# Feed-forward: the convolution's right tap as a diagonal float32 matmul at the head of TensorE's step, and VectorE scaling one chunk ahead instead of two

## What is computed

```python
def bit_linear(x, w):                 # act_quant: 8 bits by row; weight_quant: -1, 0, 1
    xq = act_quant(x)
    wq = weight_quant(w)
    return jnp.einsum('bsd,hd->bsh', xq, wq)

h = bit_linear(layernorm(x), w1)      # 512 -> 2048
h = depthwise_conv1d(h.transpose(0, 2, 1), conv_w, conv_b)   # 3 taps along the sequence, padding 1
h = silu(h.transpose(0, 2, 1))
x = x + bit_linear(h, w2)             # 2048 -> 512
```

## Time and profile before

| | |
|---|---|
| median of 3 runs | 3316.15 us (3313.43 to 3318.39) |
| the profiled execution: time / span | 3314.49 us / 3312.7 us |
| granted TensorE clock, mean over the span | 0.893 |
| busy in the span: TensorE / VectorE / ScalarE / GpSimd | 2574.8 / 1853.1 / 1203.9 / 910.4 us |
| rounds 0 to 8 of this feed-forward | about 649 to 1160 us of the span |

### The profile page before, as it was taken

One profiled execution on the slowest core, in us unless ns is written; L12 is line 12 of the kernel. 1 busy time (PEld: TensorE's weight loads), 2 busy tenths in 40 slices (PEclk: granted clock), 3 DMA queues, 4 the chain that ended last, 5 costly groups with the idle time before them and its releaser, 6 DMA issues. The chain is left out here.

```text
span 3312.7 us, 44462 instructions
## 1 busy us (share of the span) xinstructions
PE 2574.8 (78%) x14146; PEld 1327.2 (40%) x14147; DVE 1853.1 (56%) x2672; ACT 1203.9 (36%) x1807; POOL 910.4 (27%) x741
## 2 busy tenths in 40 slices
PE   8377777356666658888887509999999999999970
PEld 4244444122232234444444204444444444444430
DVE  4477776789889676676664642223233333332225
ACT  2233333287887655555554421111111111111110
POOL 0010100066776711111111170005055311350017
PEclk9788888678888879999998859999999999999995
DMA  9560000100000020000000361003033211220018
GB/s 217 119 238 8 7 8 5 51 0 1 1 0 0 0 63 9 9 8 8 11 8 14 117 225 42 32 32 108 32 108 103 76 62 50 89 95 32 32 52 274
DMA packets 118043, 194.11 MB, mean 59 GB/s; under 512 B 55264, under 2 KB 55264, under 8 KB 117456
## 3 DMA queue, kind: packets, MB, share of 16 engines
q1 hardware_dynamic: 92607, 102.96, 11.4%
q0 software_dynamic: 25360, 90.21, 8.0%
HBM read 122.65 MB, written 70.48 MB: 58 GB/s over the span
## 5 line engine op out<-in xcount | busy, mean ns | idle before, releaser
L1806 PE MATMUL e_gate_up<-weights,e_x_t 128*128 x3456 | 772.2, 380 | 1.4 <-ACT e_x_t L1860 1.4
L1806 PEld LDWEIGHTS e_gate_up<-weights,e_x_t 128*128 128x128 bf16 x3456 | 332.8, 98 | 377.4 <-issue 5.1
L1893 DVE TENSOR_TENSOR e_mid<-e_gate,e_gate_up 128x512 f32<-128x512 f32 x144 | 98.9, 687 | 645.8 <-ACT e_gate L1866 645.8
L1826 PE MATMUL e_out<-weights,e_mid_t 128*128 x1728 | 384.7, 379 | 1.1 <-DVE e_mid_t L1906 1.1
L1866 ACT ACTIVATE e_gate<-e_gate_up 128x512 f32<-128x512 f32 x144 | 86.0, 597 | 684.6 <-PE e_gate_up L1806 684.6
L559 PE MATMUL a_turn<-a_wo,a_mixed_t 128*128 128x512 bf16 (+1 forms) x1024 | 284.9, 435 | 2.4 <-DVE a_mixed_t L817 1.7
L1826 PEld LDWEIGHTS e_out<-weights,e_mid_t 128*128 128x128 bf16 x1728 | 169.0, 98 | 204.8 <-issue 1.2
L492 POOL TENSOR_TENSOR a_probs<-a_e,a_probs 128x616 bf16<-128x616 f32 x64 | 85.6, 1353 | 516.4 <-ACT a_probs L726 516.4
L1015 POOL TENSOR_TENSOR f_shared<-f_shared 128x512 f32<-128x512 f32 x128 | 181.0, 1415 | 124.4 <-DVE f_shared L1293 124.4
L1085 PE MATMUL f_out<-f_w,hidden 128*128 128x512 f16 x512 | 143.7, 409 | 91.2 <-ACT hidden L1187 90.7
L650 ACT ACTIVATE a_probs_t<-a_flip 77x512 f32<-77x512 f32 (+1 forms) x256 | 192.3, 801 | 53.7 <-PE a_flip L508 53.6
(11 more groups left out here) (239 smaller groups left out, 4279.8 us busy)
## 6 DMA issues: line engine op xcount, KB each, us to landing
raw_weights<-in_w POOLq DMA_DIRECT2D x72, 512.0 KB, 4.0
sorted_x<-a_zero_row POOLq DMA_DIRECT2D x1, 18432.0 KB, 55.9
e_x_rows<-sorted_x SPq DMA_DIRECT2D x72, 256.0 KB, 2.7
sorted_y<-e_y_rows SPq DMA_DIRECT2D x72, 256.0 KB, 2.0
raw_weights<-in_w SPq DMA_DIRECT2D x24, 512.0 KB, 4.0
x<-in_x SPq DMA_DIRECT2D x4, 2048.0 KB, 21.7
out<-x SPq DMA_DIRECT2D x32, 256.0 KB, 4.1
hidden<-in_w_t SPq DMA_DIRECT2D x1, 4096.0 KB, 14.4
```

The costliest lines, as they stand in the source:

```text
L1806: last = nc.tensor.matmul(gate_up[half][:, part, :], x_t[:, u, a, k, :], plan.weights13[:, bass.ds(expert % 2, 1), b, k, col:col + 512], s ...
L1826: last = nc.tensor.matmul(out[:, :], mid_t[:, a, j, :], plan.weights2[:, bass.ds(expert % 2, 1), b, j, :], start=(j == 0 and a == b == 0), ...
L1893: nc.vector.tensor_tensor(mid[:, half, :], gate[:, half, :], gate_up[half][:, 1, :], ALU.mult).then_inc(mid_made, 1)
```

## The change

The right tap leaves ScalarE and GpSimd's addition and becomes one float32 matmul per chunk: a 128 by 128 diagonal matrix of the chunk's right weights times `padded`, shifted by one position, into a bank `right` of its own. It is the first thing of a chunk's step on TensorE. It waits for its own chunk to be scaled down and for the left tap of the chunk before, which reads the same bank. VectorE's left tap now reads that bank in place of y, and writes y. ScalarE's centre tap goes to `side`; the activation of the right tap is gone. GpSimd adds y and side as before, and also waits for the centre tap. VectorE scales down chunk j+1 in step j, not j+2. `front` gives up its bank and shares `scales_bank`; the two transposes stand one step later. GpSimd makes the 16 diagonals once, behind the quantising of w2, in memory that is then free.

```diff
+        diagonals = shared[:, 0:HC * P].rearrange("p (c n) -> p c n", c=HC)
...
-        front = pb("front", [P, 2, 512], F16)
+        right = pb("right", [P, 512])
         scales_bank = pb("scales_bank", [P, 512])
+        front = scales_bank[:, :].bitcast(F16).rearrange("p (i n) -> p i n", i=2)
...
+            pool.wait_ge(small_in, 32)
+            pool.wait_ge(weights_made, 2)
+            for j in range(HC):
+                nc.gpsimd.tensor_scalar(diagonals[:, j, :], core.ident[:, :], conv_w[:, j, 2:3], None, ALU.mult
+                                        ).then_inc(diagonals_made, 1)
...
                         pool.wait_ge(left_added, HC * b + j + 1)
+                        pool.wait_ge(taps_made, HC * b + j + 1)
...
+            def right_tap(b, j):
+                if isinstance(b, int) and b == 0:
+                    pe.wait_ge(diagonals_made, j % HC + 1)
+                pe.wait_ge(scaled_down, HC * b + j + 1)
+                at_least(pe, left_added, HC * b + j)
+                nc.tensor.matmul(right[:, :], diagonals[:, j % HC, :], padded[:, j % BUF, 2:S + 2],
+                                 start=True, stop=True).then_inc(right_ready, 1)
...
                 for j in range(HC + LAG):
+                    if has_middle and j < HC:
+                        right_tap(b, j)
                     if has_middle and j + 2 < HC:
                         first(b, j + 2, parity)
...
-                    if has_front and j in (8, 11):
-                        flip(b + 1, j // 11)
+                    if has_front and j in (9, 12):
+                        flip(b + 1, j // 12)
...
-                nc.scalar.activation(y[:, j % BUF, :], padded[:, j % BUF, 1:S + 1], ACT.Identity,
-                                     bias=column(conv_b, j % HC), scale=conv_w[:, j % HC, 1:2])
-                nc.scalar.activation(side[:, j % BUF, :], padded[:, j % BUF, 2:S + 2], ACT.Copy,
-                                     scale=conv_w[:, j % HC, 2:3]).then_inc(taps_made, 1)
+                nc.scalar.activation(side[:, j % BUF, :], padded[:, j % BUF, 1:S + 1], ACT.Identity,
+                                     bias=column(conv_b, j % HC), scale=conv_w[:, j % HC, 1:2]
+                                     ).then_inc(taps_made, 1)
...
-                    if has_middle and j + 2 < HC:
-                        scale_down(b, j + 2, parity)
+                    if has_middle and j + 1 < HC:
+                        scale_down(b, j + 1, parity)
...
-                        dve.wait_ge(taps_made, HC * b + j + 1)
+                        dve.wait_ge(right_ready, HC * b + j + 1)
+                        at_least(dve, hidden_made, HC * b + j + 1 - BUF)
                         nc.vector.scalar_tensor_tensor(y[:, j % BUF, :], padded[:, j % BUF, 0:S],
-                                                       conv_w[:, j, 0:1], y[:, j % BUF, :], ALU.mult, ALU.add
+                                                       conv_w[:, j, 0:1], right[:, :], ALU.mult, ALU.add
                                                        ).then_inc(left_added, 1)
```

More of the change, by code:

```diff
@@ L959, in ffn @@
         product_ready = sem("product_ready"); scaled_down = sem("scaled_down")
+        diagonals_made = sem("diagonals_made"); right_ready = sem("right_ready")
         taps_made = sem("taps_made"); left_added = sem("left_added"); right_added = sem("right_added")
@@ L1029, in flip @@
                 pe.wait_ge(rounding, TPS * n + 2 * pair + 2)
+                if pair == 0:
+                    pe.wait_ge(row_copied, n + 1)
                 at_least(pe, front_copied, TPS // 2 * n + pair)
@@ L1051, in _ @@
                 flip(0, pair)
-            pe.wait_ge(row_copied, 1)
+            pe.wait_ge(front_copied, TPS // 2)
             weight_sums(1)
@@ L1057, in _ @@
             last.then_inc(columns_ready, 1)
-            pe.wait_ge(front_copied, TPS // 2)
             def first(b, j, parity):
@@ L1104, in iteration @@
                     pe.wait_ge(tops_made, b + 1)
-                    at_least(pe, row_copied, b + 1 + has_front)
+                    pe.wait_ge(front_copied, TPS // 2 * (b + 1 + has_front))
                     for i in range(TPS):
@@ L1255, in _ @@
             dve.wait_ge(zeroed, 8)
+            dve.wait_ge(small_in, 32)
             def scale_down(b, j, parity):
@@ L1265, in _ @@
             scale_down(0, 0, 0)
-            scale_down(0, 1, 0)
             def iteration(b, parity, has_middle, has_back, has_front):
@@ L1284, in iteration @@
                 for j in range(HC):
-                    if has_middle and j + 2 < HC:
-                        scale_down(b, j + 2, parity)
+                    if has_middle and j + 1 < HC:
+                        scale_down(b, j + 1, parity)
                     elif has_front:
-                        if j + 2 == HC:
-                            dve.wait_ge(row_copied, b + 2)
-                        scale_down(b, j + 2, 1 - parity)
+                        dve.wait_ge(row_copied, b + 2)
+                        scale_down(b, j + 1, 1 - parity)
                     if has_middle:
-                        dve.wait_ge(taps_made, HC * b + j + 1)
+                        dve.wait_ge(right_ready, HC * b + j + 1)
+                        at_least(dve, hidden_made, HC * b + j + 1 - BUF)
                         nc.vector.scalar_tensor_tensor(y[:, j % BUF, :], padded[:, j % BUF, 0:S],
-                                                       conv_w[:, j, 0:1], y[:, j % BUF, :], ALU.mult, ALU.add
+                                                       conv_w[:, j, 0:1], right[:, :], ALU.mult, ALU.add
                                                        ).then_inc(left_added, 1)
```

## The result

| | before | changed |
|---|---|---|
| median | 3315.8 us (4 runs, 3313.43 to 3318.39) | 3346.55 us (4 runs, 3344.26 to 3354.71) |
| ratio | | 1.0097, 95% interval 1.0078 to 1.0116 |
| profiled execution, time / span | 3314.49 / 3312.7 us | 3345.43 / 3343.5 us |
| granted TensorE clock | 0.893 | 0.900 |

A second measurement beside later experiments gave 1.0093 (1.0076 to 1.0110). The change makes the kernel 31 us slower, where the forecast said 19.

What follows compares the result with a forecast made beforehand. TensorE's 2.59 us step cannot catch up behind VectorE's three long jobs. Rounds 2 to 6 +13.8, round 1 +1.6, round 7 +3.4: +18.8 on 3314.49 gives 3333.3, plus 1.7 for the median, 3335 us; range 3312 to 3360, own range 3323 to 3350.

Steps and rivals of the forecast that it cites:

- the walk: Round 5 timed step by step from the row copy: last left tap ends at 53.01 us, not 49.97; round 64.65 us.
- The costs of the parts: Per chunk: right tap 0.86 us, result after 1.03; left tap 0.75 instead of 1.20; GpSimd's additions 1.24 instead of 1.44.
- the diagonals: GpSimd makes 16 before round 0's first left tap: taken as nothing, at most 5 us.
- the clock falls in the new waits: Rival: two slow stretches of eight matmuls per round, 1.73 us each, over seven rounds: +24, 3359 us; chance 0.15.
- +13.8 us: Rounds 2 to 6 together: 64.65 us each against 61.89, +2.8 each.
- Round 7: No scales job; last left tap ends near 49.7 us, round takes 61.3 us against 57.93: +3.4.
- round 1: No residual additions hold VectorE, left tap 0 comes earlier, giving back some 1.2 of 2.8 us: +1.6.
- VectorE's waits: Sign of being right: VectorE stands idle before its left tap until TensorE.
- No change: Rival: the walk is too strict by 3 us a round, so 3316 us; chance 0.16.
- the slow left tap: Rival: left tap stays at 1.2 us beside GpSimd, 1.8 us a round: 3348 us; counted within the forecast's 0.55.
- The right tap is cheap: Rival: diagonal matmul under 0.61 us makes the kernel faster; at 0.43, 3299 us; chance 0.14 with any other gain.
- The Trainium skill's figure: 131 ns per 512-column matmul: TensorE's step an estimated 1.6 us, GpSimd the bound, kernel faster; given no chance.

Runs made afterwards that it cites:

- Filling the third wait: Changed kernel with 12 repeated TensorE matmuls in the 3.00 us wait before right tap 14, behind VectorE's third long job, in rounds 1 to 6: ratio 1.0075.
- the first wait filled as well: Changed kernel with repeated matmuls before right tap 14 and one more repeat of first(b, 2) before right tap 1, rounds 1 to 7: ratio 1.0070.
- a tap of 0.22 us: Changed kernel with the right tap as one bfloat16 matmul on the upper 16 bits of padded, less exact: ratio 0.9999.
- The longer tap: Changed kernel with each right tap made twice into the same bank, 1.72 us instead of 0.86: ratio 1.0325.
- eleven of sixteen taps: Changed kernel with eleven chunks' right taps on TensorE, the others as before the change; first ahead of right tap, VectorE two chunks ahead: 0.9911, 3281.36 us.
- all sixteen, in the same order and with the same lead: Changed kernel with the right tap behind first in each TensorE step and VectorE scaling down two chunks ahead: ratio 1.0082.
- one of them alone: Changed kernel with only VectorE's scaling down moved to two chunks ahead, the right tap still ahead of first: ratio 1.0439.

## Why the prediction was right, and what it missed

**The bound and the walk.** The walk through round 5 gave times from the row copy. VectorE's left taps in the trace of the changed kernel (chunks 0, 3, 4, 7, 8, 11, 12, 13, 14, 15; the copy is at 973.45):

```profile
977.54 0.74 DVE L1314 SCALAR_TENSOR_TENSOR f_shared<-f_padded,f_conv_w,f_right 128x512 f32<-128x512 f32 x1
...
985.59 0.75 DVE L1314 SCALAR_TENSOR_TENSOR f_shared<-f_padded,f_conv_w,f_right 128x512 f32<-128x512 f32 x1 [1.03 <-PE f_right L1085]
...
990.22 0.73 DVE L1314 SCALAR_TENSOR_TENSOR f_shared<-f_padded,f_conv_w,f_right 128x512 f32<-128x512 f32 x1
...
997.40 0.75 DVE L1314 SCALAR_TENSOR_TENSOR f_shared<-f_padded,f_conv_w,f_right 128x512 f32<-128x512 f32 x1 [1.03 <-PE f_right L1085]
...
1003.56 0.74 DVE L1314 SCALAR_TENSOR_TENSOR f_shared<-f_padded,f_conv_w,f_right 128x512 f32<-128x512 f32 x1
...
1011.25 0.75 DVE L1314 SCALAR_TENSOR_TENSOR f_shared<-f_padded,f_conv_w,f_right 128x512 f32<-128x512 f32 x1 [1.03 <-PE f_right L1085]
...
1013.84 0.75 DVE L1314 SCALAR_TENSOR_TENSOR f_shared<-f_padded,f_conv_w,f_right 128x512 f32<-128x512 f32 x1 [1.03 <-PE f_right L1085]
...
1020.68 0.74 DVE L1314 SCALAR_TENSOR_TENSOR f_shared<-f_padded,f_conv_w,f_right 128x512 f32<-128x512 f32 x1
...
1023.64 0.75 DVE L1314 SCALAR_TENSOR_TENSOR f_shared<-f_padded,f_conv_w,f_right 128x512 f32<-128x512 f32 x1 [1.63 <-PE f_right L1085]
...
1028.31 0.75 DVE L1314 SCALAR_TENSOR_TENSOR f_shared<-f_padded,f_conv_w,f_right 128x512 f32<-128x512 f32 x1 [2.27 <-PE f_right L1085]
```

| left tap | walk | measured |
|---|---|---|
| 0 | 4.10 | 4.09 |
| 3 | 12.06 | 12.14 |
| 4, behind the scales | 17.31 | 16.77 |
| 7 | 24.41 | 23.95 |
| 8, behind the maxima | 30.65 | 30.11 |
| 12 | 40.79 | 40.39 |
| 13, behind the maxima | 47.75 | 47.23 |
| 15 | 52.26 | 54.86 |

Up to left tap 13 no step is off by more than 0.6 us, and that came with the scales job, 0.6 us shorter than in the trace of before (3.36 against 3.96). From tap to tap within a piece it is 2.59 us (1011.25 to 1013.84 for taps 11 and 12), TensorE's 12 slots of 0.216. The costs of the parts were right: 0.86 us for the right tap (1.02 to its visible end), 0.75 for the left tap, GpSimd no longer slowed. A cost taken as nothing, the diagonals, was small: GpSimd makes them in 9.35 us from 644.95, and the weight loads of the first two right taps waited 1.1 us for them together. Up to the end of round 0 2.3 us came in all, 0.8 of them before its first left tap, and that time alone differs by up to 5.8 us between traces of kernels that are alike up to there (648.34 to 654.09).

**What failed** is the last piece, and the step of the prediction is the rival "the clock falls in the new waits", which stood beside the forecast with 0.15 instead of in its sum. Left tap 15 came 2.6 us late, because right tap 14 and the eight matmuls behind it ran at half speed, and right tap 15 in part (1.46 us). Over rounds 2 to 6 the forecast had +13.8 us and +25.1 came. So the walk gives the direction and a little over half of what the rounds lost, and the rest is a mechanism that the sum had at nothing; that the time still fell inside the range, near its upper end, owes something to luck, because that range was not drawn for the clock. Filling the third wait won back 1.7 of the missing 2.3 us a round. With the first wait filled as well, the rounds were as long as the walk had them (64.37 and 64.65 us). The rival's own price, 24 us, was for two slow stretches of eight matmuls a round; 2.3 us is 1.3 of them.

**Two smaller steps.** Round 7 has a slip in its sum: 53.01 less the scales job (23.31 - 21.32 = 1.99) and the transposes of step 9 (0.45) is 50.57, not 49.7, so the walk gives +4.3 there and not +3.4; two traces have +5.3 and +3.0. For round 1 the forecast had +1.6, and the traces have +1.2 and +5.0.

**The signs.** Of what was named as a sign of being right, the 256 records, VectorE's waits, left taps of 744 ns and GpSimd's 1.27 us came. The row copies were to lie 64 to 65 us apart and lie 66.9 apart, and TensorE waits four times a round, not three, because the first wait was not counted.

**The rivals.** No change and the slow left tap are out by the rows. "The right tap is cheap" is out as a fact, since it costs what a full float32 matmul does (0.86 us from 1015.81 to 1016.67). Its price was wrong too: it had 12 taps on the path and a break-even at 0.61 us per tap, but with a tap of 0.22 us the kernel only reaches the time of before. A shorter tap won what 7 taps are worth, with slow matmuls behind right tap 1 in every round. The longer tap cost what 9.2 are worth against the changed kernel, and 11.8 against the walk, at a higher granted clock. So the count of 12 was right as far as these runs tell, and the clock, which the price left out, works against a change of the tap either way.

**The Trainium skill's figure** of 131 ns per matmul, *TensorE: Matmul & The Clock Gate*, "Back-to-back issue gap", would have made the change a gain by the prediction's estimate; the rows after show 216 ns, as those of before did (four matmuls from 1016.67 to 1017.53).

## What to carry to other kernels

Before moving work to the engine that is least busy, ask how long its step becomes beside the others' and whether it can catch up behind their long jobs; an engine with 26% of idle time may have none at the place where it is awaited. A part of the work may be the right amount: eleven of sixteen taps gave 0.9%, where all sixteen, in the same order and with the same lead, cost 0.8%. An order and a lead are tuned together, and one of them alone can cost 3%.

## What had not been expected of the hardware

Twelve superfluous matmuls of 512 columns in a wait of 3.0 us made rounds 2 to 6 1.7 us shorter each on average (65.25 against 66.91 us), because the matmuls behind the wait then ran at 2.4 GHz, not 1.2 (1.03 us for four, not 1.91). And in one kernel, on one engine, the same operation took 741 ns with an operand in PSUM and 1315 ns with both in SBUF while GpSimd worked there; in round 0 of the kernel before, without GpSimd beside it, it took 740 ns with both in SBUF too.
